# A mixture-of-experts stage whose 128-slot tiles are worked on first instead of every fourth

## The reference, cut to what matters

```python
# x: 3125 x 256; D, H, E = 256, 512, 8
xf = _layernorm(x)
probs = softmax(xf @ gate_w + gate_b)
top2_vals, top2_idx = top_k(probs, 2)
for e in range(8):
    h = gelu(xf @ W1[e] + b1[e])          # 3125 x 512
    y = h @ W2[e] + b2[e]                 # 3125 x 256
    out += cw[:, e] * y                   # cw is 0 where e is not among a row's two
x = x + out
```

## Time and profile before

| what | value |
| --- | --- |
| median of 3 runs | 1334.64 us (1334.37 to 1336.47) |
| the profiled execution, its own time | 1334.33 us |
| its span from first to last instruction | 1332.6 us |
| PE busy | 1242.6 us (93%) |
| DVE busy | 570.0 us (43%) |
| ACT busy | 473.7 us (36%) |
| POOL busy | 198.2 us (15%) |
| expert stage, first gather to last instruction | 1098.10 to 1332.6 us |

### The profile page before, as it was taken

How to read it: one execution, slowest core, us unless ns; L and a number is a source line. 1 busy time by engine, 2 the same in 40 slices (tenths; PEclk the granted TensorE clock), 3 DMA queues, 4 the chain that set the end, 5 groups by cost and what they waited for, 6 DMA issues and landing times. The chain is left out here.

```text
span 1332.6 us, 19869 instructions
## 1 busy us (share of the span) xinstructions
PE 1242.6 (93%) x7442; PEld 844.6 (63%) x7442; DVE 570.0 (43%) x1529; ACT 473.7 (36%) x1142; POOL 198.2 (15%) x201
## 2 busy tenths in 40 slices
PE   3399999989999999999999999999999878999995
PEld 1277777745558544457777544467777547888884
DVE  5878777567764413123333333222222471222221
ACT  5765666357743787830000010001222302222221
POOL 3000000023310000000000000000000005767773
PEclk8599999999999999999999999999999889999998
DMA  5132133400003155575556445587653264666662
GB/s 178 38 124 73 56 121 125 139 28 0 1 0 126 43 157 155 154 157 126 124 128 140 128 148 149 152 188 168 143 120 68 64 198 136 146 142 149 157 156 44
DMA packets 253597, 154.91 MB, mean 116 GB/s; under 512 B 172536, under 2 KB 242375, under 8 KB 253364
## 3 DMA queue, kind: packets, MB, share of 16 engines
q1 hardware_dynamic: 242420, 138.56, 38.0%
q0 software_dynamic: 11072, 14.97, 6.1%
HBM read 78.48 MB, written 35.00 MB: 85 GB/s over the span
## 5 line engine op out<-in xcount | busy, mean ns | idle before, releaser
L974 PE MATMUL bank<-weights,agg_in_out 128*128 128x320 f16 x2000 | 274.8, 299 | 0.0
L988 PE MATMUL bank<-weights 128*128 128x512 f16 x1250 | 270.7, 379 | 1.2 <-issue 1.2
L974 PEld LDWEIGHTS bank<-weights,agg_in_out 128*128 128x128 f16 x2000 | 195.7, 98 | 76.2
L988 PEld LDWEIGHTS bank<-weights 128*128 128x128 f16 x1250 | 122.0, 98 | 149.3 <-DVEq L1786 1.7
L1111 PE MATMUL bank<-weights,agg_in_out 128*128 128x320 f16 x1000 | 163.2, 299 | 0.0
L804 POOL TENSOR_TENSOR shift<-shift,rstd 128x5 f32<-128x5 f32 x15 | 3.6, 243 | 914.6 <-ACT rstd L809 914.6
L519 ACT CAST weights<-bank 128x500 f16<-128x500 f32 x160 | 114.2, 723 | 68.9 <-PE bank L508 68.9
L1111 PEld LDWEIGHTS bank<-weights,agg_in_out 128*128 128x128 f16 x1000 | 91.7, 98 | 26.2
L2258 PE MATMUL bank<-weights 128*128 x448 | 105.5, 384 | 0.5 <-ACT weights L2274 0.2
L2274 ACT ACTIVATE weights<-bank,weights 128x256 f32<-128x256 f32 (+1 forms) x128 | 50.2, 444 | 155.4 <-PE bank L2243 155.4
L2243 PE MATMUL bank<-wk,weights 128*128 128x256 f32 (+1 forms) x512 | 104.2, 357 | 0.9 <-DVE wk L2289 0.9
(11 more groups left out here) (355 smaller groups left out, 1455.8 us busy)
## 6 DMA issues: line engine op xcount, KB each, us to landing
weights<-counts_source_target SPq DMA_DIRECT2D x50, 800.0 KB, 4.6
counts_source_target<-weights SPq DMA_DIRECT2D x5, 4000.0 KB, 13.9
weights<-in_L_ffn_W SPq DMA_DIRECT2D x32, 512.0 KB, 3.9
weights<-in_L_ffn_W SPq DMA_DIRECT2D x4, 1024.0 KB, 5.5
rows_and_gates<-normed SPq DMA_DIRECT2D x1, 3300.0 KB, 12.0
out<-residual SPq DMA_DIRECT2D x1, 3072.0 KB
residual<-in_x SPq DMA_DIRECT2D x4, 640.0 KB, 7.9
weights<-in_L_ffn_b SPq DMA_DIRECT2D x1, 1024.0 KB, 7.6
```

The costliest lines, as they stand in the source:

```text
L974: last = nc.tensor.matmul(bank, source[:, 5 * k + c, part * F + fh * P:part * F + fh * P + P], MB[:, k, c, h * HALF:(h + 1) * HALF], start ...
L988: last = nc.tensor.matmul(ps[j][:, :], MB[:, k, c, j * P:(j + 1) * P], source[:, 5 * k + c, :], start=(k == 0 and c == 0), stop=(k == 4 an ...
```

## The change

The eight narrow tiles become tiles 0 to 7 of the order and the 24 wide ones tiles 8 to 31. Entries of `tile_i`, `row_i` and `out_i` stay where they are, so every slot is computed as before, only at another place in the order. TensorE's wait for gathered rows needs the number of DMAs that have filled buffer `n % 4` so far; before, all tiles of one buffer were of one kind, and now they are not, so the number is summed by `gathered(n)` when the program is built.

```diff
         def is_narrow(n):
-            return n % 4 == 3
+            return n < NARROW
 
         def parts(n):
             return 1 if is_narrow(n) else 2
 
         def numbered(n):
-            return WIDE + n // 4 if is_narrow(n) else 3 * (n // 4) + n % 4
+            return WIDE + n if is_narrow(n) else n - NARROW
 
         def first_half(n):
-            return 2 * WIDE + n // 4 if is_narrow(n) else 2 * numbered(n)
+            return 2 * WIDE + n if is_narrow(n) else 2 * numbered(n)
...
+        def gathered(n):
+            return 16 * sum(parts(j) for j in range(n % 4, n + 1, 4))
...
                 def turn(n):
-                    pe.wait_ge(x_ld[n % 4].sem, 16 * parts(n) * (n // 4 + 1))
+                    pe.wait_ge(x_ld[n % 4].sem, gathered(n))
```

## The result

The changed kernel is slower: 1338.17 us median (1336.03 to 1341.72, 12 runs) against 1335.43 (1333.98 to 1336.62, 12 runs), a ratio of 1.0022 with a 95% interval of 1.0013 to 1.0031. The forecast was 1331.3, with 1329.2 to 1335.8 as range; forecast was faster, and 0.13 was given to slower. In ten further runs it was 1339.35, ratio 1.0029 (1.0017 to 1.0041). Its runs also spread more: 5.7 us, against 2.6 before.

The account below looks back on a forecast made before the run. TensorE was taken to bound the middle, with POOL's serial scatters next, and waits the two ends. Terms -5.2 + 1.5 + 0.4 = -3.3 us took the profiled 1334.33 to 1331.0, plus 0.3 for the median: 1331.3, range 1329.2 to 1335.8.

Parts of the forecast that it names:

- The sum: Whole kernel: last product 5.2 us earlier, wait for POOL 1.5, tail 0.4, together -3.3 us.
- The tail: After the last product: a wide last tile's two scatters land 8.1 us later, against 7.7 before, so +0.4.
- The start: Tile 0: needs one gather, first product at 1103.2, finished at 1108.1 instead of 1115.6, 7.5 us earlier.
- the beat: TensorE in the narrow tiles: 3.8 us when a narrow one follows, 0.18 saved on each of six, -1.1.
- the wait: TensorE at the turn to tile 8: waits for a gather behind POOL's serial scatters, taken as 1.5 us.
- rival (d): Narrow tiles: scatters land in 5.2 us each and decide, TensorE loses 8.0, slower at 1337.8 us; chance 0.13.
- Rival (b): Start: the clock falls as it did before, 1.7 us paid, 1333.0 us; chance 0.14.
- My argument from the shorter gaps: Start: new gaps of 0.8, 0.6 and 0.9 us are shorter than one of 2.1 that left the clock full.
- The formula: POOL in narrow tiles: each scatter's beat is its landing plus 0.85 us; tile 8's gathers follow the fifth scatter.
- the point from which it turns: Narrow tiles: slower where the wait passes 4.8 us, at a mean scatter beat of 5.25, a landing of 4.4.
- VectorE's wait for scatters: Narrow tiles: scatter 4 lands 7.7 us after its tile ends, 9.8 allowed, so the copy behind is not late.
- rival (c): Narrow tiles: weight loads of 5.9 us decide, beat 4.1, gathers late too, about 1333.5 us; chance 0.09.

Follow-up runs that it names:

- first profile: Profiled execution of the changed kernel from its first measurement: 236.0 us from first gather to end, 234.5 in the kernel before; median 1338.17 us.
- second profile: Profiled execution of the changed kernel measured again without edit: 238.8 us from first gather to end; median 1339.35 us, ratio 1.0029 to the kernel before.
- the run in the middle: Changed kernel reordered to twelve wide tiles, the eight narrow ones in a row, twelve wide: 1341.68 us, ratio 1.0046 to the kernel before.
- 24 products: 24 products of zeros ahead instead of 18: changed kernel 1337.58 us; narrow-wide-wide-wide order with early gelu table and empty slots' gathers left out 1333.90 us.

## Why the prediction was wrong, step by step

**Which step failed.** The sum was -5.2 + 1.5 + 0.4. The tail was right: +0.36 against +0.4. The start, the beat and the wait were each too low, by 1.9, 1.0 and 1.8 us in the first profile. These are 4.7 of the 4.8 us between -3.3 and the +1.5 of the stage; the median moved by 2.7. The term that failed is the wait for POOL's serial scatters, put at 1.5 us and measured as 3.3 and 7.1 (5.4 without what the clock cost). The mechanism of the wait was named at its place (scatter after scatter, then the gather of tile 8, waited for at the turn), but its size was off by a factor of two to four, since the landings of the scatters were taken from rows with fewer loads beside them; and rival (d), slower by that mechanism, was given 0.13.

**The start, 1.9 too low.** I had the first product at +5.1 and tile 0 finished, that is the next first product begun, at +10.0. It began at +5.8 in both profiles, because the first gather landed in 4.7, not 4.1 as the first one of the earlier trace rows. Most of that, 0.5, comes from empty slots that all read one row (4.2 with them left out). In the first profile tile 0 was finished at +11.9, in the second, with a full clock, at +11.0. Rival (b), the clock, came true in four of the nine profiles that begin with a narrow tile and have as many products ahead. Its price was 0.9 at tile 0 and not 1.7, since ScalarE's table load fills part of the same time: TensorE idled 0.44 us ahead of the second product at the low clock and 1.08 at the full one. My argument from the shorter gaps did not hold: gaps of 1.5 and 0.6 us were enough at times, where one of 2.1 us was not the earlier trace rows.

**The beat, 0.16 too low.** I let a narrow tile followed by a narrow one save 0.18 of the 0.22 that two transposes less are worth. The beat is 3.96, as before: the second product then begins when the gelu of the first pair is there, with 0.2 of idle time ahead of its weight loads (in tile 2 that gelu ends at 1117.72, and the loads begin at 1117.96). Nearly 1.0 us over six tiles. It was bounded rightly (0 to 0.22), and the wrong end was taken. The trace of before had the answer: the wide tile that begins at 1201.46 has only two transposes in its turn, and the next tile begins at

```profile
1208.88 1.97 PEld L2243 LDWEIGHTS bank<-wk,weights 128*128 128x128 f32 x16
```

which is 7.42 us later, as with four transposes. The sum also counted only the six turns that become cheaper, and not the eight wide tiles before narrow ones that lose their short turn; at 0.22 each these would have outweighed the six.

**The wait, 1.5 against 3.3 and 7.1.** The formula was sound: with scatter landings of the earlier trace rows the fifth scatter was to start 17.15 after the first, and without weight loads, where the landings of tiles 1 to 3 are again 3.1, 3.8 and 3.9, it starts 17.3 after it. In the change it is 20.3 and 21.2, because the landings are 3.6, 4.5, 3.7 and 5.0 to 5.8, not 2.8, 3.2, 3.8 and 3.8. I had seen that the loads would come every 3.8 us instead of every 6.55 and put 0.5 us on the whole wait for it. The runs show 3 us and more on four landings. The sign of the forecast hung on that, and the point from which it turns, a mean landing of 4.4, was in the text: the first four landings are 4.2 and 4.4 on average, and the losses at start and beat did the rest. A low clock after a wait in the run, 1.7 us in the second profile, was not in the sum at all. Nor was VectorE's wait for scatters, which the prediction had as not late yet: the scatter of tile 3 landed at 1133.5, when VectorE had wanted to begin tile 5's add a microsecond earlier. In the first profile this cost TensorE nothing, with earlier gathers it did.

**Rule and trace.** The Trainium skill, "TensorE: Matmul & The Clock Gate", What's actually happening, has the throttled state as the default, which activity lifts. The runs agree so far as the clock was at 0.50 at the start of four of nine profiles, after gaps of 1.5 to 1.9 and of 0.6 us. The Trainium skill, "DMA: Bandwidth & Descriptors", SWDGE vs HWDGE vs iDMA, has the DMAs of SyncE and GpSimd in different queues that the 16 engines serve in turn. The runs agree: tile 3's scatter landed in 5.0 and 5.8 us with the loads and in 3.9 without. Both rules spoke against the change.

**What was right.** TensorE's beat in the wide part is 7.42 with no wait, no weight load was waited for (rival (c)), the tail is 0.4 longer, and the ends do gain where the run is avoided, though 1.6 us in the profiles and not 3.3.

## What to carry to other kernels

A serial chain that is hidden on average (here POOL's scatters, one per tile, behind TensorE) is hidden by the mix of tiles: sort the short tiles together and its beat has to hold against the shortest tile alone. When a reordering raises the rate of loads, take the landing times from the row's upper half and not from the neighbours of the same kind, for these were measured beside a lower rate. And look at what a run of one kind costs apart from what the ends gain: moving one short tile to the front, and with it a wide one to the end, gave all of the gain.

## What the runs showed of the hardware

- A gather of 128 rows is slower when most indices are the same row. The eight narrow gathers of the kernel before landed in 3.9, 3.6, 3.0, 2.9, 3.4, 3.4, 3.7 and 3.7 us; counted from the reference's choice of experts, the narrow tiles hold 1, 31, 89, 128, 53, 40, 0 and 0 rows, and the rest of their slots read row 0. The fuller the tile, the sooner it landed, but for the first. Reading distinct rows instead took the first gather from 4.7 or more to 4.3, nearly as much as not reading at all (4.2). At the start it holds up the gathers behind it too: the four of tiles 0 to 3 landed in 4.8, 6.1, 5.8 and 4.8 us in the change, in 4.3, 5.0, 4.4 and 3.4 with distinct rows, and in 4.2, 4.2, 3.5 and 2.8 with empty slots left out, though tile 3 is full in all three. Later it matters less: the gathers of tiles 6 and 7, which hold no row, landed in 4.4 and 4.3, 4.3 and 4.1, and 4.0 and 3.8.
- A 512 KB load every 4 us lengthens some scatters and not others: those of tiles 1, 2 and 3 landed in 4.5, 3.7 and 5.0 us (4.6, 3.7 and 5.8 in the second profile) with it, and in 3.1, 3.8 and 3.9 without loads.
- The same program started its first tile at the full clock in some executions and at the low one in others. Of the 11 profiles of kernels with 18 products ahead, six have 0.50 at the start (the kernel before and the first profile of the change among them), for some 3 us in five and for nearly 7 in the run in the middle; five have 1.00 (the second profile of the change among them), and so have the two with 24 products.
- What a wait of TensorE does to the clock was not settled by its length. At the turn to tile 8 a wait of 1.8 us (first profile of the change) left it at 1.00, one of 2.1 (24 products ahead) and one of 4.2 (second profile) were followed by 1.2 GHz, and in the run in the middle so were three of 0.9, 1.8 and 3.0 within 20 us. In the earlier trace rows a gap of 2.1 us left it at 1.00.
